# All layer norms: GpSimd takes the variance to the power of minus one half, in place of reciprocal, root and correction

## The reference

```python
def _layernorm(x, axis=-1, eps=1e-05):
    m = jnp.mean(x, axis=axis, keepdims=True)
    v = jnp.var(x, axis=axis, keepdims=True)
    return (x - m) / jnp.sqrt(v + eps)
...
x = x + _L0_xattn_ref(ctx_1024, _layernorm(x, axis=-1), ...)
x = x + _L0_attn_ref(_layernorm(x, axis=-1), ...)
x = x + _L0_ffn_ref(_layernorm(x, axis=-1), ...)
x = x + _L1_xattn_ref(_layernorm(x, axis=-1), ctx_1024, ctx_1024, ...)
x = x + _L1_attn_ref(_layernorm(x, axis=-1), ...)
x = x + _L1_ffn_ref(_layernorm(x, axis=-1), ...)
```

## Time and profile before

| | before |
|---|---|
| median of 3 runs | 2055.04 us (2054.64 to 2056.28) |
| the profiled execution | 2053.8 us, its span 2051.7 us |
| TensorE busy in the span | 1718.3 us |
| VectorE busy | 1594.6 us |
| ScalarE busy | 1504.4 us |
| GpSimd busy | 908.9 us |

### The profile page before, as it was taken

How to read it: one execution, slowest core, us unless ns; L and a number is a source line. 1 busy time by engine, 2 the same in 40 slices (tenths; PEclk the granted TensorE clock), 3 DMA queues, 4 the chain that set the end, 5 groups by cost and what they waited for, 6 DMA issues and landing times. The chain is left out here.

```text
span 2051.7 us, 51500 instructions
## 1 busy us (share of the span) xinstructions
PE 1718.3 (84%) x13455; PEld 1392.9 (68%) x13455; DVE 1594.6 (78%) x4998; ACT 1504.4 (73%) x4156; POOL 908.9 (44%) x1339
## 2 busy tenths in 40 slices
PE   3599999999999999971710679999999799749997
PEld 3489999999999999941500356666667566427775
DVE  4798888888888888837788669999999588636664
ACT  3488888888888888854765479999999588545553
POOL 1544444444444444304156034444444377335554
PEclk8599999999999999995755799999999799879998
DMA  4277676777777777610000059999999300103322
GB/s 139 85 167 165 160 160 157 161 163 162 159 162 163 159 160 164 151 42 0 0 0 0 2 147 250 252 250 251 249 249 248 73 1 0 32 13 102 91 87 82
DMA packets 196234, 259.54 MB, mean 127 GB/s; under 512 B 25136, under 2 KB 141328, under 8 KB 196032
## 3 DMA queue, kind: packets, MB, share of 16 engines
q1 hardware_dynamic: 194678, 256.53, 50.0%
q10 hardware_dynamic: 1194, 1.58, 0.3%
q0 software_dynamic: 288, 0.56, 0.1%
HBM read 86.09 MB, written 4.72 MB: 44 GB/s over the span
## 5 line engine op out<-in xcount | busy, mean ns | idle before, releaser
L778 ACT ACTIVATE a_prob<-a_neg,a_nmax 128x289 f32<-128x289 f32 x512 | 266.6, 525 | 1.4 <-DVE a_nmax L705 1.1
L840 PE MATMUL a_out<-a_probT,a_xn 128*128 128x256 f32 x1024 | 263.0, 380 | 5.0 <-DMA a_probT<-a_blocks 4.2
L1710 ACT ACTIVATE b_prob<-b_neg,b_nmax 128x257 f32<-128x257 f32 x512 | 260.6, 515 | 6.9 <-DVE b_nmax L1661 6.8
L671 POOL TENSOR_TENSOR a_xn<-a_z,g 128x256 f32<-128x256 f32 x128 | 93.8, 733 | 384.6 <-DVE a_z L739 384.6
L830 PE MATMUL a_score<-a_xnT,a_qT 128*128 128x290 f32 x1536 | 252.9, 314 | 2.5 <-DVE a_qT L750 2.5
L705 DVE CUSTOM_DVE_ANT_0 a_neg<-a_score,a_bias 128x289 f32<-128x289 f32 x512 | 211.6, 458 | 41.2 <-PE a_score L830 36.8
L786 ACT ACTIVATE a_prob<-a_prob,a_rinv 128x289 f32<-128x289 f32 x512 | 231.3, 527 | 1.8 <-DVE a_rinv L755 1.7
L830 PEld LDWEIGHTS a_score<-a_xnT,a_qT 128*128 128x128 f32 x1536 | 222.3, 190 | 9.6 <-issue 3.3
L1661 DVE CUSTOM_DVE_ANT_0 b_neg<-b_score,b_bias 128x257 f32<-128x257 f32 x512 | 188.6, 419 | 30.5 <-PE b_score L1801 15.3
L840 PEld LDWEIGHTS a_out<-a_probT,a_xn 128*128 128x128 f32 x1024 | 175.2, 191 | 19.8 <-DMA a_probT<-a_blocks 5.3
L716 DVE STREAM_TRANSPOSE a_blocks<-a_prob 128x1024 f32<-128x1024 f32 x128 | 159.4, 1245 | 24.0 <-ACT a_prob L786 17.7
(11 more groups left out here) (478 smaller groups left out, 4567.9 us busy)
## 6 DMA issues: line engine op xcount, KB each, us to landing
a_probT<-a_blocks SPq DMA_DIRECT2D x512, 192.0 KB, 3.6
b_probT<-b_blocks SPq DMA_DIRECT2D x256, 256.0 KB, 4.6
a_raw<-in_ctx SPq DMA_DIRECT2D x128, 128.0 KB, 2.9
b_raw<-in_ctx SPq DMA_DIRECT2D x64, 256.0 KB, 4.7
m_wide<-expert_weights SPq DMA_DIRECT2D x128, 128.0 KB, 2.9
a_kept<-keep SPq DMA_DIRECT2D x32, 257.0 KB, 3.4
b_kept<-keep SPq DMA_DIRECT2D x32, 257.0 KB, 4.8
b_v_rows<-ctx_tail_values SPq DMA_DIRECT2D x32, 256.0 KB, 4.7
```

The costliest lines, as they stand in the source:

```text
L778: nc.scalar.activation(prob[:, par, grp, 0:KEYS0], neg[:, grp, :], ACT.Exp, bias=nmax[:, par, grp:grp + 1], scale=-1.0, accum_out=rsum[:, ...
L840: nc.tensor.matmul(out_ps[:, half, 0:2 * P], xn[:, j, kt, :], probT[:, u, 2 * half:2 * half + 2, kt, :], start=(kt == 0), stop=False)
L1710: nc.scalar.activation(prob[:, (j + 5) % 4, grp, :], neg[:, par, grp, :], ACT.Exp, bias=nmax[:, par, grp:grp + 1], scale=-1.0, accum_out=r ...
```

## The change

VectorE computes the variance plus epsilon as before, with the mean now behind it in VectorE's order, and signals GpSimd. GpSimd takes that tile to the power of -0.5 in one instruction, with the first column of `k.minus_half` repeated as the exponent, and VectorE waits for the result. Reciprocal, ScalarE's root and the three instructions of the correction are no longer there; ScalarE has no part in `ln_stats`. The square of the means' difference waits for that difference alone.

```diff
--- before.py
+++ after.py
@@ -80,9 +80,8 @@
     tile = lambda part: stack.enter_context(nc.sbuf_tensor(f"{name}_{part}", [P, n], F32))
     stats = k.stats[:, 0:n]
     mean, rstd, twice = tile("mean"), tile("rstd"), tile("twice")
-    mean_sum, mean_diff, var, var_eps, inv, error, inner = (tile(part) for part in (
-        "mean_sum", "mean_diff", "var", "var_eps", "inv", "error", "inner"))
-    chain, inv_ready, root_ready = k.sem(f"{name}_chain"), k.sem(f"{name}_inv_ready"), k.sem(f"{name}_root_ready")
+    mean_sum, mean_diff, var, var_eps, inner = (tile(part) for part in ("mean_sum", "mean_diff", "var", "var_eps", "inner"))
+    chain, var_ready, root_ready = k.sem(f"{name}_chain"), k.sem(f"{name}_var_ready"), k.sem(f"{name}_root_ready")
     with nc.Block() as block:
 
         @block.vector
@@ -95,41 +94,29 @@
             nc.vector.tensor_tensor(mean_diff[:], stats[:, :, 1], stats[:, :, 4], ALU.subtract).then_inc(chain, 1)
             nc.vector.tensor_tensor(var[:], stats[:, :, 2], stats[:, :, 5], ALU.add).then_inc(chain, 1)
             nc.vector.tensor_tensor(mean_sum[:], stats[:, :, 1], stats[:, :, 4], ALU.add).then_inc(chain, 1)
-            dve.wait_ge(chain, first + 3)
+            dve.wait_ge(chain, first + 1)
+            nc.vector.scalar_tensor_tensor(mean_diff[:], mean_diff[:], 0.25, mean_diff[:], ALU.mult, ALU.mult).then_inc(chain, 1)
+            dve.wait_ge(chain, first + 4)
+            nc.vector.scalar_tensor_tensor(var[:], var[:], 1.0 / D, mean_diff[:], ALU.mult, ALU.add).then_inc(chain, 1)
+            dve.wait_ge(chain, first + 5)
+            nc.vector.tensor_scalar(var_eps[:], var[:], EPS, None, ALU.add).then_inc(var_ready, 1)
             nc.vector.tensor_scalar(mean[:], mean_sum[:], 0.5, None, ALU.mult).then_inc(chain, 1)
-            nc.vector.scalar_tensor_tensor(mean_diff[:], mean_diff[:], 0.25, mean_diff[:], ALU.mult, ALU.mult).then_inc(chain, 1)
-            dve.wait_ge(chain, first + 5)
-            nc.vector.scalar_tensor_tensor(var[:], var[:], 1.0 / D, mean_diff[:], ALU.mult, ALU.add).then_inc(chain, 1)
-            dve.wait_ge(chain, first + 6)
-            def rsqrt(root, n, before):
-
-
-                nc.vector.tensor_scalar(var_eps[:], var[:], EPS, None, ALU.add).then_inc(chain, 1)
-                dve.wait_ge(chain, before + 1)
-                nc.vector.reciprocal(inv[:], var_eps[:]).then_inc(inv_ready, 1)
-                dve.wait_ge(root_ready, n)
-                nc.vector.tensor_tensor(error[:], root[:], root[:], ALU.mult).then_inc(chain, 1)
-                dve.wait_ge(chain, before + 2)
-                nc.vector.scalar_tensor_tensor(error[:], error[:], -0.5, var_eps[:], ALU.mult, ALU.mult).then_inc(chain, 1)
-                dve.wait_ge(chain, before + 3)
-                nc.vector.scalar_tensor_tensor(root[:], error[:], 1.5, root[:], ALU.add, ALU.mult).then_inc(chain, 1)
-                dve.wait_ge(chain, before + 4)
-
-            rsqrt(rstd, 1, first + 6)
+            dve.wait_ge(root_ready, 1)
             if extra is not None:
                 nc.vector.tensor_tensor(inner[:], rstd[:], rstd[:], ALU.mult).then_inc(chain, 1)
-                dve.wait_ge(chain, first + 11)
+                dve.wait_ge(chain, first + 7)
                 nc.vector.tensor_tensor(var[:], var[:], inner[:], ALU.mult).then_inc(chain, 1)
-                dve.wait_ge(chain, first + 12)
-                rsqrt(twice, 2, first + 12)
+                dve.wait_ge(chain, first + 8)
+                nc.vector.tensor_scalar(var_eps[:], var[:], EPS, None, ALU.add).then_inc(var_ready, 1)
+                dve.wait_ge(root_ready, 2)
                 nc.vector.tensor_tensor(twice[:], twice[:], rstd[:], ALU.mult).then_inc(chain, 1)
-                dve.wait_ge(chain, first + 17)
-
-        @block.scalar
-        def _(act):
-            for n, root in enumerate((rstd,) if extra is None else (rstd, twice)):
-                act.wait_ge(inv_ready, n + 1)
-                nc.scalar.activation(root[:], inv[:], ACT.Sqrt).then_inc(root_ready, 1)
+                dve.wait_ge(chain, first + 9)
+
+        @block.gpsimd
+        def _(pool):
+            for r, root in enumerate((rstd,) if extra is None else (rstd, twice)):
+                pool.wait_ge(var_ready, r + 1)
+                nc.gpsimd.tensor_tensor(root[:], var_eps[:], k.minus_half[:, 0:1].broadcast_to([P, n]), ALU.pow).then_inc(root_ready, 1)
     return (mean, rstd) if extra is None else (mean, rstd, twice)
```

## The result

The changed kernel takes 2087.19 us (median of 4 runs, 2085.05 to 2087.68), the kernel before 2055.66 us in the same session (2054.64 to 2057.42). The ratio is 1.0148 with a 95% interval of 1.0136 to 1.016: 31.5 us more by the medians, 30.4 by the ratio, 28 to 33 by its interval. The forecast was 2096.5 within 2057 to 2104, slower with 0.80. The profiled execution took 2087.68 us, its span is 2085.6.

What follows compares the result with a forecast made beforehand. At the norms between stages one chain running alone was taken as the bound. Pows of 51.6 us less 9.86 and 0.3 gave +41.5 us, so 2095.3 for the profiled execution and 2096.5 for the median, within 2057 to 2104.

Steps and rivals of the forecast that it cites:

- What bounds the kernel there: At the layer norms between stages one chain runs alone, so a microsecond on it is one of the kernel.
- The credit: Time saved at the norms before paying for pows: 1.42 us per 32-column norm, 2.76 in lat_ln, 9.86 in all.
- The price of the pow: GpSimd's seven pows in the norms, priced mostly by the column from one two-column row: 51.6 us in all.
- X: Duration of one GpSimd pow in a norm: 7.31 us for 32 columns, 7.53 for 33.
- the linear one: Forecast case for the norms' pows: 150 ns a column and more, 2081 to 2103 us, chance 0.50.
- the middling price: Rival for the norms' pows: 43 to 150 ns a column, for example 2071 us, chance 0.28.
- The table loads: Nine ScalarE loads go, hidden but for one in attn1; rival with loads on the path: 2085 us, chance 0.02.
- The 0.3 us in attn1: Credit for attn1's first Exp, which started late behind a table load that the change removes.
- GpSimd's code: lat_ln's first pow follows a configuration instruction; nothing added, against some 5 us by the skill's rule.
- TensorE's clock: Already at the 1.2 GHz level at the first transposes behind r_ln and f_ln; longer idle time takes nothing more.

Runs made afterwards that it cites:

- e3: The changed kernel with each pow made twice, the first into a spare tile: 2125.68 us, ratio 1.0344 to the kernel before.
- e2: The changed kernel with a multiplication in place of each pow, normalised values wrong: 2048.04 us, ratio 0.9966 to the kernel before.
- e1: The changed kernel with extra GpSimd pows of 1 to 64 columns and plain multiplications in the setup: 2112.46 us, a single run.
- e4: The changed kernel with ScalarE's square roots put back beside the pow, into a tile nobody reads: 2085.89 us, ratio 1.0151 to the kernel before.
- e5: The kernel before with the changed form in f_ln and m_ln alone: 2066.01 us, ratio 1.0051.
- e8: The kernel before with only the mean moved behind the reciprocal and the square started earlier, ScalarE's root kept: 2055.29 us, ratio 1.0000.
- e6: The kernel before with the changed form in lat_ln, r_ln, b_ln and s_ln: 2079.50 us, ratio 1.0112.

## Why the prediction was right

**What bounds the kernel there** was right: one chain on VectorE and a helper engine, with nothing beside it. e3 shows it best, where 38.5 us more of pow are 38.5 us more of time.

**The credit** was right to some hundredths in the trace (3.96 for 4.00 in r_ln, 12.61 for 12.61 in lat_ln), and e2 bears it out in the whole time.

**The price of the pow** is the term that was off in size. I put 0.05 us of the 0.49 on set-up and 220 ns on each column, X = 7.31; e1 gives 388 ns once and 157 a column, and the trace 5.42. The extra of a two-column pow over a plain operation is thus 0.2 us of set-up and 0.3 of columns, a mix that the one width in the trace could not tell. The seven pows take 38.5 us, not 51.6. That is -13.1 of the forecast's +41.5, leaving 28.3; the measured +31.5 has some 3 us more, or 2 by the ratio, which I had not forecast and which made the miss smaller. By the forecast's cases it is the linear one, but only just: 157 ns a column, where the middling price began below 150. That case was told from its neighbour by luck, for the 0.05 us of set-up was a choice, and the trace had one width.

**The table loads** cost nothing, as the idle times had said, and e4 shows it. The rule of the Trainium skill (ScalarE: Activation LUTs, "What ACT_TABLE_LOAD costs") that a switch of sets costs about 2.66 us is not what the traces show. The load is 1.28 us in every one, and around the load of the earlier trace rows ScalarE's work ends at 1629.18 + 1.27 = 1630.45 and the Exp starts at 1631.76, so the whole switch took 1.31 us. And nine of them came back in e4 for no measurable time. The 0.3 us in attn1 was seen in its place (the Exp waits for VectorE alone) and is too small to show in the whole. The row ahead of the load, before:

```profile
1629.18 1.27 ACT L1959 ACTIVATE s_spread<-s_keys,head_of_feature 128x128 f32<-128x128 f32 x4
```

**GpSimd's code** had no start-up that shows: 38.8 to 40.25 us lay under VectorE's chain. The rule of the Trainium skill (GPSIMD Engine Reference, "Instruction dispatch") that a first call to freshly loaded code costs about 6 us is not borne out by any row here: the first pow in e1 took 729 ns, 17 more than the median of the earlier trace rows. Whether the configuration instructions load fresh code in this program, no row shows.

**TensorE's clock** was the weak step, though not in the way that its sentence would suggest. "A longer idle time takes nothing more" is right at the transposes behind r_ln and f_ln, which run at the 1.2 GHz level as before, and e5 bears it out for all of ffn0: 4 us more of idle time ahead of it and a rest of 199.0. What the forecast left out is that the clock's rise later in a stage is not fixed to the work. In ffn0 it comes later behind the changed norms of the stages ahead, for 1 to 2 us; in moe1 the rest moves by up to 2.5 us with and without a pow. Of the 3 us some 1 to 2 are thus found in ffn0, and the rest can't be told from the scatter of single executions. The cause of the later rise stays open.

## What to carry to other kernels

An operation whose price for each further column is not known must be priced at two widths before it is moved: one row at two columns fitted a pow of 0.8 us and one of 8 us at 32. Where a short chain runs alone between two barriers, count what each step hands over, work out the break-even duration (here 1.41 us, that is six columns of GpSimd's pow), and only then choose the engine. A table load that falls into ScalarE's idle time costs nothing that shows, as the nine here. And a slow operation whose first part is enough to start the consumer can be cut into pieces and hidden.

## What was not expected of the hardware

- GpSimd's pow costs 0.39 us and 157 ns for each column of 128 partitions, with the same duration for a constant, for real data, for one exponent or many; a plain multiplication of 32 columns is 241 ns.
- A width of 33 costs 0.26 to 0.44 us more than one of 32 (5.68 in the kernel, 5.86 in e1), more than one column's price; 31 and 32 are on the line.
- VectorE's subtractions of 128x128 keep their 341 ns beside GpSimd's pow, though two of those in attn1 that start beside a GpSimd multiplication of 128x1536 (2.77 us) take 1.25 and 1.04 us and end within 0.1 us of its end.
- moe1 with the same root and the same matmuls takes from 281.8 to 284.4 us, with TensorE busy 230.5 to 233.8 us, by when its clock changes level. In the third ten us of the stage the granted clock is 1.00 before and 0.75 in e8, with 36 matmuls against 30.
- ffn0, whose own norm and work are the same in both, takes 199.2 us before and 201.3 in e6, with the norms of the stages ahead changed.
